# All keys and values projected in the prologue, and the attention's normalised query input on GpSimd, in a two-layer gated cross-attention kernel

## What is computed

```python
x = x + tanh(g_xattn[0]) * wkv(time_decay, time_first, k=layernorm(x), v=ctx)       # a scan over the 128 positions
x = x + tanh(g_ffn[0])   * ffn0(layernorm(x))     # (silu(x @ gate.T * gs) * (x @ up.T * us)) @ down.T * ds, 704 hidden
x = x + tanh(g_xattn[1]) * attention(layernorm(x), ctx, mask, mask)
    # in each batch 128 channels x 256 tokens; 16 heads of 8; q = Wq t + bq, k = Wk s + bk, v = Wv s + bv
    # dot = mask * (q k / sqrt(8)) - (1 - mask) * 1e6; softmax(dot) * mask @ v
x = x + tanh(g_ffn[1])   * moe(layernorm(x))      # top-1 of 8 experts with capacity 256, and a shared expert
```

## Time and profile before

| | us |
|---|---|
| three timed runs | 583.60, 587.51, 588.49; median 587.51 |
| the profiled execution, its own time | 581.58 |
| its span in the profile | 579.8 |

### The profile page before, as it was taken

One profiled execution on the slowest core, in us unless ns is written; L12 is line 12 of the kernel. 1 busy time (PEld: TensorE's weight loads), 2 busy tenths in 40 slices (PEclk: granted clock), 3 DMA queues, 4 the chain that ended last, 5 costly groups with the idle time before them and its releaser, 6 DMA issues. The chain is left out here.

```text
span 579.8 us, 10728 instructions
## 1 busy us (share of the span) xinstructions
PE 487.7 (84%) x3400; PEld 269.2 (46%) x3400; DVE 397.8 (69%) x871; ACT 243.7 (42%) x478; POOL 217.8 (38%) x353
## 2 busy tenths in 40 slices
PE   1149999999696769899988888888779999899994
PEld 1034564747353424333343343333233555578883
DVE  4989879695336778888888888887755733333331
ACT  1132233121231048777777777777741001123331
POOL 2526234231283235555555555531301370024334
PEclk9999999999997969999999999999899999999998
DMA  5901007630267054655555555450004024157873
GB/s 139 334 2 36 1 6 119 88 43 0 73 179 191 20 135 131 154 157 145 140 154 144 144 145 144 125 128 5 5 2 149 32 105 138 55 126 194 195 151 36
DMA packets 68246, 61.94 MB, mean 107 GB/s; under 512 B 8992, under 2 KB 63248, under 8 KB 68208
## 3 DMA queue, kind: packets, MB, share of 16 engines
q1 hardware_dynamic: 65136, 57.25, 37.8%
q0 software_dynamic: 3072, 4.21, 4.3%
HBM read 39.01 MB, written 22.43 MB: 106 GB/s over the span
## 5 line engine op out<-in xcount | busy, mean ns | idle before, releaser
L1008 DVE TENSOR_REDUCE MX<-psum 128x2 f32<-128x512 f32 x256 | 166.3, 681 | 31.6 <-PE psum L874 31.5
L1086 ACT ACTIVATE HP<-psum 128x512 f32<-128x512 f32 x256 | 138.6, 600 | 43.6 <-PE psum L880 42.9
L874 PE MATMUL psum<-QKA 60*128 60x256 bf16 x512 | 82.0, 279 | 18.3 <-DVE MX L1008 16.7
L880 PE MATMUL psum<-QKA 60*128 60x256 bf16 x512 | 80.0, 277 | 9.4 <-ACT HP L1086 7.4
L953 PE MATMUL psum<-HP,VP 128*32 128x256 f32 x1024 | 82.9, 397 | 0.2 <-ACT HP L1086 0.2
L437 PE MATMUL psum<-space_a,space_w 128*128 128x512 f32 x160 | 72.8, 606 | 4.1 <-PEq L497 2.4
L874 PEld LDWEIGHTS psum<-QKA 60*128 60x128 bf16 x512 | 35.3, 95 | 64.9 <-DVE MX L1008 47.8
L1656 POOL DMA_INDIRECT out_x<-OE,to_u x16 | 25.0, 1562 | 72.6 <-ACT OE L1697 70.2
L437 PEld LDWEIGHTS psum<-space_a,space_w 128*128 128x128 f32 x160 | 29.8, 193 | 40.4 <-issue 34.4
L1795 PE MATMUL psum<-XT,WE 128*128 128x256 f32 (+1 forms) x192 | 44.1, 380 | 1.6 <-ACT XT L1681 1.6
L1721 PE MATMUL psum<-space_a,wsh 128*128 (+3 forms) x96 | 42.8, 595 | 0.8 <-PEq L1224 0.8
(11 more groups left out here) (183 smaller groups left out, 739.8 us busy)
## 6 DMA issues: line engine op xcount, KB each, us to landing
QKA<-stack_scr SPq DMA_DIRECT2D x32, 480.0 KB, 5.4
stack_scr<-PARTS SPq DMA_DIRECT2D x32, 192.0 KB, 2.1
WE<-in_W SPq DMA_DIRECT2D x16, 352.0 KB, 4.0
stack_scr<-PARTS SPq DMA_DIRECT2D x32, 128.0 KB, 1.9
XD<-dispatched SPq DMA_DIRECT2D x8, 258.0 KB, 3.7
X<-in_x SPq DMA_DIRECT2D x4, 512.0 KB, 5.5
CV<-in_ctx SPq DMA_DIRECT2D x4, 512.0 KB, 3.6
CX<-in_ctx SPq DMA_DIRECT2D x16, 128.0 KB, 5.1
```

The costliest lines, as they stand in the source:

```text
L874: return pe.matmul(to[:, tt * T:(tt + 1) * T], QKA[rows, k, 0, h, tt * P:(tt + 1) * P], QKA[rows, k, 1, h, :], start=True, stop=True)
L880: return pe.matmul(to[:, (j % 2) * T:(j % 2 + 1) * T], QKA[rows, k, 1, h, st * P:(st + 1) * P], QKA[rows, k, 0, h, :], start=True, stop=True)
L1008: dve.tensor_reduce(MX[:, par, head_of(n), :], src[:, :].rearrange("p (a s) -> p a s", a=2), axis=AX.X, op=ALU.max).then_inc(a_red, 1)
L1086: act.activation(PT[:, i % 2, st, 2 * half:2 * half + 2, :].rearrange("p j t -> p (j t)"), TBK3[THIRDS[m]], ACT.Exp).then_inc(a_exp, 1)
```

## The change

The context of all 16 batches is loaded at the start (`CTX`), and TensorE projects it in 16 units (`pe_keys_values`): an even unit the keys of two batches, an odd one their values. ScalarE copies them to `KR` (with the bias) and `VR`, which stay to the end of the attention. Twelve units stand between the transposes into and out of the scan of group 0, four behind the latter. The transposes of the second half of group 0 get banks 2 and 3 (`WB2`). Key and value products, the key's bias, `dve_vf`, `pe_v` and the context load go from the attention; GpSimd adds the value bias in `pool_vp` and masks key and query in two operations. Z3 is made by GpSimd (`pool_z3`), right behind `power_step`, in two operations in place of VectorE's one.

In the prologue the loads have a new order; five small ones that the scan needs are issued by ScalarE; the product of `dw` and `dsb` moves from VectorE to GpSimd (`s_dw`), between the sums and the quotients of group 0. The three mask parts and the scaling of `wq` move to VectorE's last group. In `dve_group` the reciprocal of the first half stands behind the step i = 0. TensorE's loop over the groups is written out. SyncE's 14 mask-row DMAs and its wait for them are as before.

The diff, cut (`+` and `-` lines of renamed semaphores and declarations are left out):

```diff
+            KR = sbp("KR", [P, B, T])
+            VR = sbp("VR", [P, B, 2, P])
+            CTX = sbw("CTX", [P, B, C])
...
+            KV = [bank[6], bank[7]]
+
+            def pe_keys_values(pe, u):
+
+                j, side = divmod(u, 2)
+                if u == 0:
+                    pe.wait_ge(s_wkv, 32)
+                if side == 0 and j % 2 == 0:
+                    pe.wait_ge(s_c[j // 2], 16)
+                if u == 1:
+                    pe.wait_ge(s_mT2, 1)
+                if u >= 2:
+                    pe.wait_ge(s_keep, u - 1)
+                if side == 0:
+                    last = pe.matmul(KV[0][:, :], wk[:], CTX[:, 2 * j:2 * j + 2, :].rearrange("p b t -> p (b t)"),
+                                     start=True, stop=True)
+                else:
+                    for b in range(2):
+                        for st in range(2):
+                            last = pe.matmul(KV[1][:, (2 * b + st) * P:(2 * b + st + 1) * P],
+                                             CTX[:, 2 * j + b, st * P:(st + 1) * P], wv[:], start=True, stop=True)
+                last.then_inc(s_pr, 1)
+
+            def act_keys_values(act, u):
+                j, side = divmod(u, 2)
+                act.wait_ge(s_pr, u + 1)
+                if side == 0:
+                    act.activation(KR[:, 2 * j:2 * j + 2, :].rearrange("p b t -> p (b t)"), KV[0][:, :], ACT.Identity,
+                                   bias=bqk[:, 1:2]).then_inc(s_keep, 1)
+                else:
+                    act.activation(VR[:, 2 * j:2 * j + 2, :, :].rearrange("p b s c -> p (b s c)"), KV[1][:, :],
+                                   ACT.Copy).then_inc(s_keep, 1)
...
-            N_SMALL, N_ROWS = 15, 14
+            N_CHAIN, N_SMALL, N_ROWS = 5, 10, 14
+            N_UNITS, N_FIRST = B, 12
...
+                    load_x(0)
+                    load_ctx(0)
+                    sp.dma_start(mrow[:], mask).then_inc(s_mask, 16)
+                    for dst, src in ((wk[:], wkT), (wv[:], wvT)):
+                        sp.dma_start(dst, src).then_inc(s_wkv, 16)
+                    load_ctx(1)
+                    load_ctx(2)
+                    load_x(1, s_xb)
+                    load_ctx(3)
...
-                    with sp.Fori(2, NG) as g:
-                        sp.wait_ge(s_vT, 1 + 2 * g)
-                        load_ctx(g)
-
-
                     sp.wait_ge(s_mp, 1)
...
-                    act.wait_ge(s_ld, 16 * N_SMALL)
+                    chain = [(td[:], time_decay), (tf[:], time_first),
+                             (gates[:, 0:2], g_xattn.partition_broadcast(P)), (gates[:, 2:4], g_ffn.partition_broadcast(P)),
+                             (bqk[:, 1:2], bk)]
+                    assert len(chain) == N_CHAIN
+                    with nc.allow_non_contiguous_dma(reason="small vectors"):
+                        for dst, src in chain:
+                            act.dma_start(dst, src).then_inc(s_chain, 16)
+                    act.wait_ge(s_chain, 16 * N_CHAIN)
...
                     act_exps(act, 0, 0)
-                    act_exps(act, 0, 1)
+                    act_exps(act, 0, 1, WB2)
+                    for u in range(N_UNITS):
+                        act_keys_values(act, u)
+                    act_z1(act, 1)
+                    act_zt(act, 0)
+                    act_exps(act, 1, 0)
                     act.wait_ge(s_dv0, 3)
-                    act_z1(act, 1)
-                    act_exps(act, 1, 0)
-                    act_zt(act, 0)
...
+                    pool.wait_ge(s_wts, 80)
+                    pool.wait_ge(s_ld, 16 * N_SMALL)
+                    pool.tensor_tensor(dw[:, :, :], dw[:, :, :], dsb[:, :].unsqueeze(1).broadcast_to([P, NI, C]),
+                                       ALU.mult).then_inc(s_dw, 1)
...
-                    for h in range(2):
-                        pe_wkv_in(pe, 0, h)
-                    pe_wkv_out(pe, 0)
+                    pe_wkv_in(pe, 0, 0)
+                    pe_wkv_in(pe, 0, 1, WB2)
+                    for u in range(N_FIRST):
+                        pe_keys_values(pe, u)
+                    pe_wkv_out(pe, 0, WB2)
+                    for u in range(N_FIRST, N_UNITS):
+                        pe_keys_values(pe, u)
+                    pe_z2T(pe, 0)
+                    pe_wkv_in(pe, 1, 0)
                     pe.wait_ge(s_wts, 80)
-                    pe_wkv_in(pe, 1, 0)
-                    pe_z2T(pe, 0)
 
...
-                    dve.wait_ge(s_mask, 16)
-                    for j, (mul, add) in enumerate(((-NEG, 0.0), (NEG, -NEG), (-1.0, 1.0))):
-                        ch.do(dve.tensor_scalar(mtmp[:, j, :], mrow[:], mul, add, ALU.mult, ALU.add))
-
-                    def mask_part(r):
-                        ch.wait()
-                        last = dve.tensor_copy(mparts[:, :, r, :], mtmp[:, :, :])
-                        if r == 2:
-                            last.then_inc(s_mp, 1)
-                            return
-                        ch.do(last)
-                        ch.wait()
-                        ch.do(dve.tensor_tensor(mtmp[:, :, :], mtmp[:, :, :], mparts[:, :, r, :], ALU.subtract))
-
-                    mask_part(0)
-                    dve.wait_ge(s_ld, 16 * N_SMALL)
+                    dve.wait_ge(s_chain, 16 * N_CHAIN)
...
-                        dve_products(dve, 0, h)
-                        dve_scans(dve, 0, h)
+                    dve_products(dve, 0, 0)
+                    dve_scans(dve, 0, 0)
+                    dve_products(dve, 0, 1, WB2)
+                    dve_scans(dve, 0, 1)
                     for h in range(2):
                         dve_recip(dve, 0, h)
-                    mask_part(1)
                     dve_stats1(dve, ch, 1)
-                    dve_x1(dve, 0)
+                    dve_x1(dve, 0, WB2)
                     dve_ln2(dve, ch, 0)
-                    mask_part(2)
+                    dve.wait_ge(s_ld, 16 * N_SMALL)
+                    ch.do(dve.tensor_scalar(hgs[:], gs[:], 0.5, None, ALU.mult))
+                    ch.wait()
+                    dve.tensor_tensor(hgu[:], hgs[:], us[:], ALU.mult).then_inc(s_dv0, 1)
                     dve_products(dve, 1, 0)
                     dve_scans(dve, 1, 0)
-                    dve.wait_ge(s_mT, 1)
-                    dve.tensor_copy(maskT[:, :, :].rearrange("p h b -> p (h b)"), bank[7][:, 0:2 * B]).then_inc(s_mT2, 1)
...
                     def dve_group(ch, g, last):
-                        dve_recip(dve, g + 1, 0)
                         for i in range(NI):
                             dve_h1(dve, ch, g, i)
                             dve_h(dve, ch, g, i)
                             if i == 0:
+                                dve_recip(dve, g + 1, 0)
                                 dve_products(dve, g + 1, 1)
                                 dve_scans(dve, g + 1, 1)
                             if i == 1 and not last:
                                 dve_stats1(dve, ch, g + 2)
+                            if i == 1 and last:
+                                mask_lines()
+                                mask_part(0)
                             if i == 2:
                                 dve_recip(dve, g + 1, 1)
+                            if i == 3 and last:
+                                mask_part(1)
                             if i == 4:
                                 dve_x1(dve, g + 1)
                         dve_ln2(dve, ch, g + 1)
                         if not last:
                             dve_products(dve, g + 2, 0)
                             dve_scans(dve, g + 2, 0)
+                        else:
+                            mask_part(2)
+                            mch.do(dve.tensor_scalar(wq[:], wq[:], HD ** -0.5, None, ALU.mult))
+                            mch.do(dve.tensor_scalar(bqk[:, 0:1], bqk[:, 0:1], HD ** -0.5, None, ALU.mult))
                         dve_x2(dve, g, DB)
...
 
-                def dve_z3(dve, b):
+                def pool_z3(pool, pch, b):
                     n = b if isinstance(b, int) and b < GB else 0
-                    dve.wait_ge(a_rstd, LN_COUNT(b))
+                    pool.wait_ge(a_rstd, LN_COUNT(b))
                     if later(b):
-                        dve.wait_ge(a_proj, b)
-                    dve.tensor_scalar(Z3[:], xb(b), mv[:, n, 0:1], rstd[:, n:n + 1], ALU.subtract, ALU.mult).then_inc(a_z3, 1)
-
-                def dve_vf(dve, b):
-                    dve.wait_ge(a_vps, b + 1)
-                    if later(b):
-                        dve.wait_ge(a_vp, b)
-                    dve.tensor_tensor(VF[:, :, :], MISC[:, 0:T].rearrange("p (s c) -> p s c", s=2),
-                                      bvb[:, :].unsqueeze(1).broadcast_to([P, 2, P]), ALU.add).then_inc(a_vf, 1)
+                        pool.wait_ge(a_proj, b)
+                    pch.do(pool.tensor_tensor(Z3[:], xb(b), mv[:, n, 0:1].broadcast_to([P, T]), ALU.subtract))
+                    pch.wait()
```

(36 more changed lines are left out.)

174 lines of the change are left out of this document (75 added, 99 removed).

## The result

Four runs of the kernel after took 628.48 to 631.94 us, median 630.96; four of the kernel before, in the same session, 583.60 to 588.49, median 586.49. The ratio is 1.0756 (95% interval 1.0697 to 1.0815): slower by 7.6%. Forecast were 616 us and a range of 603 to 624. The profiled execution took 630.45 us against 581.58, so 48.9 us are to be found in the traces; the forecast there was 28.8.

The account below looks back on a forecast made before the run. Bounds: a latency-chain prologue, TensorE-filled groups, an attention loop with VectorE, TensorE, ScalarE and DMA nearly level. 32.8 + 1.5 − 2.0 − 3.5 = +28.8 on 581.58 gave 610.4, plus 5.9 carried over: 616 us, range 603 to 624.

Parts of the forecast that it names:

- the largest term: End of the first block: mask rows issued only after VectorE's last group, 37.2 us of rows before the attention block.
- +32.8: First block as a whole: the attention block starts at 182.0 us instead of 149.2, 32.8 us later.
- the prologue's gain of 5.4 us: Prologue: the first gate matmul starts at 37.9 us instead of 43.27, 5.4 us won.
- The opening part's −2.0: Attention before its loop: key and value work removed, Z3 slower on GpSimd; net −2.0 us, ends −3.5 and +1.5.
- The clock term of +1.5: After TensorE idles over 30 us, it works at a lower clock at first: +1.5 us, ends 0 and 3.5.
- Compute per batch: −0.35 −0.33 −0.15 +0.4: Attention loop: three savings from removed key, value and VectorE work, against Z3's longer path; about −0.45 us a batch.
- −3.5 us forecast: Attention loop: −0.3 us for each of 12 batches, a DMA chain being the second limit; ends −7 and +3.5.
- The +0.4 for Z3: Attention loop: `veps` end to fifth reduce takes 3.2 us instead of 2.80, as TensorE waits in order for Z3.
- (a): Rival, mask rows before the attention block: alone they run at 334 GB/s; 589 us, no change; chance 0.07.
- (b): Rival, attention loop: NP passes its cover, or Z3 in TensorE's order costs more; +0.3 a batch, 623 us; chance 0.11.
- (c): Rival, mask rows before the attention block: half way faster, 25 us; 604 us; chance 0.08.
- (d): Rival, loop and groups: −0.8 us a batch, groups as before, `s_mp` at 139; 605 us; chance 0.10.

Follow-up runs that it names:

- e1: The kernel after with the mask's lines and three parts back in VectorE's prologue, around the first products and scans of group 1: 596.56 us.
- e3: The kernel before with only the mask's lines and parts moved into VectorE's last group: 617.66 us, ratio 1.056.
- e5: The kernel after with each group's first reciprocal back in front of the loop over the six steps: 628.69 us.
- e4: The kernel after with GpSimd's product of `dw` behind the scan sums of group 1 instead of in front of group 0's quotients: 623.75 us.
- e2: The kernel after with Z3 made by VectorE again, in one operation at p = 1, keys and values still precomputed: 619.46 us.
- e6: The kernel after with VectorE's product RD x maskG moved ahead of the first maximum of its step: 623.70 us.
- e8: The kernel after with the edits of e1, e4, e5, e2 and e6 together: 574.44 us, ratio 0.984 to the kernel before.
- e16: The kernel after with the mask on 128 partitions, so that the fourteen mask-row DMAs take their bytes from 128 partitions instead of 16: 608.36 us.
- e11: e8 with TensorE's query projection one step later (p = 2), Z3 on VectorE: 573.84 us, ratio 0.985 to the kernel before.
- e13: e11 with the product RD x maskG back at its old place behind the first maximum: 569.46 us, ratio 0.978 to the kernel before.

## Why the prediction was right and wrong

**Right.** The direction, and the largest term: the rows leave the shadow of the groups and stand alone. They were issued at 152.27 and the block began 37.6 us later (forecast 143.8, and 38.2); from the end of the last x2 to the block it was 31.0 us (158.93 to 189.88), where the forecast has 31.6 (150.4 to 182.0). The masks' move alone costs 32.9 us by e1 and 33.7 by e3. That these stand so near the forecast's +32.8 is luck: +32.8 is the whole block, with the prologue's gain of 5.4 us set against the rows. The opening part's −2.0 came as −1.9. Of the moved reciprocal's 1.75 us a group, e5 confirms those of the last two groups (1.75 and 1.6 us); group 0 did not pay it.

The clock term of +1.5 was right in the place that it was meant for and not in its cause:

```profile
149.24 1.96 PE L437 MATMUL psum<-space_a,space_w 128*128 128x512 f32 x4 [2.35 <-PEq L497]
```

```profile
189.92 3.58 PE L485 MATMUL psum<-space_a,space_w 128*128 128x512 f32 x4 [32.43 <-PEq L546]
```

The first four passes behind the barrier took 1.6 us longer than before, but they took 3.19 us in e1 too, where TensorE had not stood still for 31 us. Over the whole attention the pause cost nothing by e1, and 2 to 3 us at most by e3.

**Wrong, first block.** The step "On GpSimd the product of `dw` (128x1536; at 1.26 us for 512 elements some 3.5 us) stands before the two quotients and makes the second end at 28.8". It counted the product's 3.5 us and not its wait for `s_ld`: of the small loads I followed only the five that had moved to ScalarE, not the ten that had moved behind the weights in SyncE's order, the last of them landing at 28.77. That made X1 6.4 us late. The first gate matmul came 7.6 us behind the forecast, which is nearly the whole miss of 7.9. e4 gives back 6.1 of the 7.6; the other 1.5 are ScalarE's normalised Z1, which the forecast had 1.4 us too early in front of ZT.

**Wrong, loop.** The step "Compute per batch: −0.35 −0.33 −0.15 +0.4". The sign was wrong: −3.5 us forecast, +7.0 measured, +0.58 a batch over 12. From the first transposed score to the experts the loop takes 224.5 us before, 231.5 after, 222.2 in e2, 222.8 in e6 and 218.1 in e8, which has neither trouble.

The largest part is in no term of the step: the product RD x maskG, 0.18 us before, 0.84 after, since GpSimd's split now starts earlier against VectorE's order. e6 prices it at 7.3 us of attention, and at 0.57 us a batch where the clock is equal.

The +0.4 for Z3 was about right in size. I compared the delay from `veps` to the fifth maximum before and after, 2.8 and 3.2 us; the rows of before, here, give 2.94, the batch above 3.33, and the medians of twelve batches are 2.94 and 3.45, so +0.51:

```profile
239.23 0.14 DVE L983 TENSOR_SCALAR veps<-mv 128x1 f32<-128x1 f32 x1
...
242.17 2.48 DVE L1008 TENSOR_REDUCE MX<-psum 128x2 f32<-128x512 f32 x4 [0.51 <-PE psum L874]
```

But a saving of VectorE inside this very stretch, whose length TensorE sets, brings nothing: the saved Z3 (0.56 us) lay there, and its removal only made VectorE wait longer, 1.41 us instead of 0.51. With Z3 back on VectorE the delay is 2.94 us again (e2 and e8, medians). The three savings together were put too high: −0.83 us a batch in the step, and −0.54 in e8 (218.1 against 224.5 us over 12 batches). In the step's own terms the runs show −0.54 +0.51 +0.57 = +0.54 us a batch, an estimate from e8, the two traces and e6, against +0.58 measured. The two losses overlap in part: e2 takes 9.3 us off the loop and e6 8.8, but e8, which has both edits, 13.5.

The granted clock may have a share too. Before, no batch of the loop was below 1.00; after, three of twelve were at 0.86 to 0.88. Windows of three neighbouring batches of the kernel after:

```profile
302.42:316.73 14.31, 11.11 (x137) 4.50 (x137) 12.26 (x28) 10.71 (x22) 9.51 (x20) 1.00 0.51 138
316.73:330.19 13.46, 11.49 (x123) 4.60 (x125) 10.72 (x24) 8.96 (x19) 8.75 (x20) 0.87 0.55 145
330.19:346.68 16.49, 12.49 (x155) 5.24 (x154) 14.46 (x33) 12.66 (x26) 10.27 (x22) 1.00 0.46 123
```

The pair of 13.46 and 16.49 us is 2 us longer than two of the three batches ahead of it (13.9 in the mean, all at 1.00). This share is argued from the windows; no run isolates it.

**The rivals.** (a) was wrong for these rows, but e16 shows it one edit away: at 224 GB/s it would have decided differently. (b), the longer loop, came true beside the main forecast, at nearly twice its price (+0.58 us a batch instead of +0.3), and only in part by its second mechanism, TensorE's order: in e6, which keeps that and frees the product, the loop is 1.8 us shorter than before, so without the held product (b) would not have come true. The later store of the maxima did not decide: the transposed scores waited 2.8 us in all for the maxima's fill, 3.2 us before. I had given it as an alternative to the forecast, though nothing in the two excludes the other: 623 us was the sum of both. (c) and (d) did not occur. No rival had the held product.

The rule that spoke against this change was at hand and not weighed. In e11 the product began 0.08 us behind GpSimd's subtraction and was out 0.04 us after it. The Trainium skill, SBUF — State Buffer (Who interferes with whom), says that a VectorE instruction with two SBUF inputs and a GpSimd instruction that reads SBUF exclude each other for the whole instruction of whichever began first; the trace agrees. The change raised GpSimd's busy time from 217.8 to 252.3 us, and each such instruction is one more that VectorE can meet.

**The best version.** e13: masks early, the `dw` product behind the sums, the reciprocal in front, Z3 on VectorE, the projection at p = 2. 569.46 us, 2.2% faster than before (1.9 to 2.6). With e16's wide rows nothing more should be had there, since early masks hide the rows anyway (in e1 SyncE waits 67.5 us for the others); that wasn't run.
